# A third region of edges summed inside the scatter stage, and pairs that follow the tiles by six steps

## The reference

```python
edge_aggr = zeros.at[src].add(edge_attr).at[dst].add(edge_attr)   # layer 0
x += relu([relu(norm(x)), edge_aggr] @ W1 + b1) @ W2 + b2
agg = segment_sum(edge_attr, dst)                                  # layer 1
x += relu([relu(norm(x)), agg] @ W1 + b1) @ W2 + b2
x += gcn(relu(gcn(norm(x))))                                       # layer 2, degree-normalised
m = relu(concat(x[src], x[dst], edge_attr) @ msg_w1 + msg_b1) @ msg_w2 + msg_b2
x += relu([x, mean_by_dst(m)] @ upd_w1 + upd_b1) @ upd_w2 + upd_b2 # layer 3
```

## Time and profile before

| | before |
|---|---|
| time, median of 3 runs | 1234.61 us (1230.02 to 1240.17) |
| profiled execution, its own time | 1233.6 us |
| its span | 1231.7 us |
| PE, DVE, ACT, POOL busy | 1099.9, 894.7, 627.8, 703.4 us |
| granted clock of TensorE, mean | 0.949 |

### The profile page before, as it was taken

One profiled execution on the slowest core, in us unless ns is written; L12 is line 12 of the kernel. 1 busy time (PEld: TensorE's weight loads), 2 busy tenths in 40 slices (PEclk: granted clock), 3 DMA queues, 4 the chain that ended last, 5 costly groups with the idle time before them and its releaser, 6 DMA issues. The chain is left out here.

```text
span 1231.7 us, 31979 instructions
## 1 busy us (share of the span) xinstructions
PE 1099.9 (89%) x9535; PEld 934.9 (76%) x9536; DVE 894.7 (73%) x3140; ACT 627.8 (51%) x1794; POOL 703.4 (57%) x720
## 2 busy tenths in 40 slices
PE   6999896999998999926887999988799999999997
PEld 3666553888887888815854899973799999999985
DVE  7889775788877879876778754465577777777763
ACT  8666544889988788766632311043133333333322
POOL 4777777777777777781000000008577777777772
PEclk9999988999999999967988999988899999999997
DMA  7674334666555666445861000027878888788951
GB/s 237 191 224 134 106 106 129 159 162 157 154 157 158 186 184 197 146 129 164 242 8 48 2 1 2 2 73 213 224 215 220 230 227 236 216 239 230 232 132 49
DMA packets 177187, 188.62 MB, mean 153 GB/s; under 512 B 44320, under 2 KB 136845, under 8 KB 176877
## 3 DMA queue, kind: packets, MB, share of 16 engines
q1 hardware_dynamic: 142086, 136.92, 42.3%
q0 software_dynamic: 22656, 46.87, 12.5%
q10 hardware_dynamic: 12264, 2.70, 1.1%
HBM read 140.19 MB, written 44.28 MB: 150 GB/s over the span
## 5 line engine op out<-in xcount | busy, mean ns | idle before, releaser
L2605 POOL DMA_INDIRECT between<-p_table,src_g x292 | 285.4, 977 | 366.2 <-DMA p_table<-n_nm 269.4
L981 POOL DMA_INDIRECT rows_by_block<-h_t,mean_bc x312 | 312.3, 1001 | 105.3 <-issue 86.5
L471 PE MATMUL acc<-ones_b 128*128 128x128 bf16 (+1 forms) x941 | 162.0, 297 | 47.6 <-PEq L911 32.9
L1112 DVE TENSOR_TENSOR between<-between,acc 128x600 f32 x208 | 161.3, 776 | 50.2 <-PE acc L1266 38.6
L1255 PE MATMUL acc<-n_nm 128*128 128x384 bf16 (+1 forms) x832 | 143.0, 295 | 34.8 <-issue 21.9
L2744 ACT ACTIVATE between<-acc 128x128 f32<-128x128 f32 x138 | 38.2, 277 | 228.0 <-PE acc L2859 204.2
L1076 DVE TENSOR_SCALAR n_nm<-iota_w,agg_sum 128x600 bf16<-128x600 f16 x416 | 144.0, 387 | 0.0
L1000 ACT ACTIVATE away<-iota_b,agg_sum 128x128 bf16<-128x128 bf16 x416 | 140.8, 385 | 0.0
L1255 PEld LDWEIGHTS acc<-n_nm 128*128 128x128 bf16 x832 | 72.6, 98 | 82.6 <-issue 26.3
L471 PEld LDWEIGHTS acc<-ones_b 128*128 128x128 bf16 x941 | 73.8, 99 | 75.6 <-issue 58.3
L2842 PE MATMUL acc<-weights,between 128*128 128x128 f32 x584 | 128.4, 302 | 0.0
(11 more groups left out here) (296 smaller groups left out, 2553.9 us busy)
## 6 DMA issues: line engine op xcount, KB each, us to landing
h_t<-in_edge_rows SPq DMA_DIRECT2D x78, 260.0 KB
between<-in_edge_columns SPq DMA_DIRECT2D x36, 512.0 KB
between<-in_dst SPq DMA_DIRECT2D x36, 288.0 KB
n_nm<-rows_by_block SPq DMA_DIRECT2D x69, 130.0 KB
h_t<-rows_by_block SPq DMA_DIRECT2D x34, 260.0 KB, 3.8
by_dst<-q_whole_table SPq DMA_DIRECT2D x138, 64.0 KB
x_nm<-rows_by_block SPq DMA_DIRECT2D x30, 260.0 KB
agg_sum<-in_edge_rows SPq DMA_DIRECT2D x26, 260.0 KB
```

The costliest lines, as they stand in the source:

```text
L471: pe.matmul(acc[:, bank * BANK + skip:(bank + 1) * BANK].rearrange("p (a n) -> p a n", n=P), ones_b[:, :], ones_b[:, :].rearrange("p (a n) ...
L981: pool.indirect_dma_start(rows_by_block, bass.IndirectOffsetOnAxis(ap=place_in_table[:, t:t + 1], axis=0), row_group(g)[:, j, :], None).th ...
L1112: dve.tensor_tensor(between[:, :, bass.ds(first, W)], between[:, :, bass.ds(first, W)], acc[:, o:o + NB * WS].rearrange("p (b w) -> p b w" ...
L2605: pool.indirect_dma_start(got[:, q, j * D:(j + 1) * D], None, p_table, bass.IndirectOffsetOnAxis(ap=src_g[:, n * G + j:n * G + j + 1], axi ...
```

## The change

The table is cut into four regions: tiles to 124, 252, 356 and 416. The third one ("mid2", blocks of five or six tiles) is now read, summed and added to `held` inside the scatter stage too, by 25 more early reads at one per pair from pair 186 to 210; the loops of that stage run eight steps past the last pair for them. The earlier reads stand closer: the wide ones in 60 pairs instead of 68, the mid ones in 46 instead of 52. The last region has two to four tiles a block, so the source stage has 25 reads. x is also loaded once in the middle of the scatter stage, for its statistics, into the space that the early reads use afterwards (the load at the end stays). ACT checks nine blocks of counts at the end of the scatter stage and three in the source stage (five and 13 before), DVE combines 13 (seven before). `held` and `agg_dst` are added at the end of the scatter stage, some small works move there too (`oddities`), and the small works of the source stage stand earlier in it; the store of the keys stands behind SP's reads, with a wait for its landing. In the last stage the pairs follow the tiles by six steps (OFF) instead of ten, rows and keys of the first four batches are loaded ahead of the stores (their buffers are now in `held`), the late chunks stand in other steps, and two waits guard their buffers.

```diff
-TILES_MID = 256
+TILES_MID = 252
 GROUPS_MID = TILES_MID // KC
+TILES_MID2 = 356
+GROUPS_MID2 = TILES_MID2 // KC
...
+def cap_mid2(b):
+    return 6 if 15 <= b < 21 else 5 if b < NB - 1 else 3
...
-    return 7 if b < 15 else 8 if b < NB - 1 else 4
+    return 3 if b < 21 else 4 if b < NB - 1 else 2
...
-CHECKED_AT_END, CHECKED_BY_ACT = 5, 18
+CHECKED_AT_END, CHECKED_BY_ACT = 9, 12
...
+                reads.append((NSB + NB + b, base_mid2(b), cap_mid2(b), True, True))
...
-            TAILS = 7
+            TAILS = 11
             READS_AFTER = 4
+            AFTER_PAIRS = 8
+            X_LOAD_AT, X_ZERO_AT, X_STATS_AT = 30, 44, 58
...
-            read_pairs = {(78 + r * 68 // wide_reads if r < wide_reads else 148 + (r - wide_reads) * 52 // NB): r for r in range(len(early_reads))}
+            def pair_of_read(r):
+                if r < wide_reads:
+                    return 78 + r * 60 // wide_reads
+                if r < wide_reads + NB:
+                    return 140 + (r - wide_reads) * 46 // NB
+                return 186 + r - wide_reads - NB
...
+                            sp.wait_ge(x_stats.h, x_stats.at(2))
...
+                        if g == X_LOAD_AT:
+                            sp.wait_ge(vec.h, vec.at(1))
+                            sp.dma_start(x_nm[:, 0:NB - 1, :], x[0:(NB - 1) * P, :].rearrange("(b p) f -> p b f", p=P)).then_inc(x_in.h, 16)
+                            sp.dma_start(x_nm[0:NLAST, NB - 1, :], x[(NB - 1) * P:N, :]).then_inc(x_in.h, 16)
...
-                    for i in range((GROUPS - READS_AFTER) * PG, PAIRS):
+                    for i in range((GROUPS - READS_AFTER) * PG, PAIRS + AFTER_PAIRS):
...
-                    for i in range(PAIRS):
-                        lows(i)
+                    for i in range(PAIRS + AFTER_PAIRS):
+                        if i < PAIRS:
+                            lows(i)
...
+                        if X_STATS_AT <= i < X_STATS_AT + 13:
+                            for b in range(2 * (i - X_STATS_AT), min(2 * (i - X_STATS_AT) + 2, NB)):
+                                ins = dve.bn_stats(stats[:, b, :], x_nm[:, b, :])
...
+                        if i == PAIRS + 2:
+                            oddities()
...
-                    dve.wait_ge(loaded.h, loaded.at(16 * 23))
-                    for b in range(NB):
-                        dve.bn_stats(stats[:, b, :], x_nm[:, b, :])
+                    dve.wait_ge(agg_read.h, agg_read.at(NSB + 2 * NB))
+                    dve.tensor_tensor(held[:, :], held[:, :], agg_dst[:, 0:NSB * SBN], ALU.add)
...
-                        if r == 2 * LB_IN:
+                        if r == LB_IN + 1:
                             count_to_nodes(sp)
-                        if r == 4 * LB_IN:
+                        if r == LB_IN + 6:
                             nodes_in(sp)
-                        if r == 24:
-                            sp.wait_ge(keys_made.h, keys_made.at(4))
-                            sp.dma_start(keys_table[0:P, :, :], turned_keys[:, 0, :, :]).then_inc(keys_out.h, 16)
-                            sp.dma_start(keys_table[P:TILES_HERE, :, :], turned_keys[0:TILES_HERE - P, 1, :, :]).then_inc(keys_out.h, 16)
+                    sp.wait_ge(keys_made.h, keys_made.at(4))
+                    sp.dma_start(keys_table[0:P, :, :], turned_keys[:, 0, :, :]).then_inc(keys_out.h, 16)
+                    sp.dma_start(keys_table[P:TILES_HERE, :, :], turned_keys[0:TILES_HERE - P, 1, :, :]).then_inc(keys_out.h, 16)
+                    sp.wait_ge(keys_out.h, keys_out.at(32))
...
-                        c = u * P
-                        dve.wait_ge(agg_read.h, agg_read.at(2))
-                        dve.tensor_tensor(agg_sum[:, c:c + P], acc[:, o:o + P], agg_sum[:, c:c + P], ALU.add).then_inc(agg_read.h, 1)
+                        c, w = u * P, min(P, NSB * SBN - u * P)
+                        ins = dve.tensor_tensor(agg_sum[:, c:c + w], acc[:, o:o + w], held[:, c:c + w], ALU.add)
+                        if w < P:
+                            ins = dve.tensor_copy(agg_sum[:, c + w:c + P], acc[:, o + w:o + P])
+                        ins.then_inc(agg_read.h, 1)
...
-                    dve.tensor_tensor(agg_sum[:, 0:NSB * SBN], held[:, :], agg_dst[:, 0:NSB * SBN], ALU.add).then_inc(agg_read.h, 1)
-                    dve.tensor_copy(agg_sum[:, NSB * SBN:NP], agg_dst[:, NSB * SBN:NP]).then_inc(agg_read.h, 1)
...
-            OFF = 10
+            OFF = 6
...
-            p_win = table_space.take([P, PWINS, 2, D])
-            rows2 = table_space.take([P, BATCHES2 * 2, KW])
-            keys2 = table_space.take([P, BATCHES2, 2 * 2 * P], U8).rearrange("p r (j k e) -> p r j k e", j=2, k=2)
+            kept_space = Space(held[:, :], F32)
+            p_win = kept_space.take([P, PWINS, 2, D])
+            rows2 = kept_space.take([P, BATCHES2 * 2, KW])
+            keys2 = kept_space.take([P, BATCHES2, 2 * 2 * P], U8).rearrange("p r (j k e) -> p r j k e", j=2, k=2)
...
-            chunks = [(4, 42), (5, 58), (6, 74), (7, 90), (8, 106), (9, 122), (0, 133), (1, 135), (2, 137), (10, 139), (3, 141)]
+            chunks = [(4, 42), (5, 58), (6, 74), (7, 90), (8, 106), (9, 122), (0, 137), (1, 138), (10, 139), (2, 140), (3, 141)]
...
+                    def p_windows(b):
+                        u, r = 2 * b, b % BATCHES2
                         if starts(b):
...
+                    sp.wait_ge(keys_out.h, keys_out.at(32))
+                    for b in range(BATCHES2):
+                        tile_rows(b)
...
                     sp.wait_ge(p_stored.h, p_stored.at(TABLE_PARTS))
-                    sp.wait_ge(keys_out.h, keys_out.at(32))
-                    tile_rows(0)
-                    tile_rows(1)
+                    for b in range(BATCHES2):
+                        p_windows(b)
                     sp.wait_ge(q_stored.h, q_stored.at(2 * TABLE_PARTS))
-                    tile_windows(0)
-                    tile_windows(1)
-                    for b in range(2, BATCHES2):
-                        tile_rows(b)
+                    for b in range(BATCHES2):
                         tile_windows(b)
...
+                            if k >= 3:
+                                dve.wait_ge(hidden.h, hidden.at(k - 2))
...
+                            if k >= 3:
+                                act.wait_ge(made.h, made.at(second_of[k - 3] + 1))
```

More of the change, by code:

```diff
@@ L314, in build @@
         bases = sb("bases", [1, 2, NK])
-        over = Space(n_flat[:, 2944:NP], F32).take([1, 6, NB])
+        over = Space(n_flat[:, 2944:NP], F32).take([1, 8, NB])
         rel2 = sb("rel2", [P, TILES_HERE])
@@ L767, in build @@
         checked = signal("checked")
+        x_in, x_stats = tabs_in, idx_read
+        late = signal("late")
         early_away = of_block = signal("of_block")
@@ new lines, in oddities @@
+                    def oddities():
+                        lower1, upper1, lower_mid, upper_mid, lower_mid2, upper_mid2 = (bounds[:, k, :] for k in (0, 1, 4, 5, 6, 7))
+                        dve.scalar_tensor_tensor(pair_far[0:1, 0:PAIRS - RING].rearrange("p (a n) -> p a n", n=RING),
+                                                 iota[0:1, 0:PAIRS // RING - 1].rearrange("p (a n) -> p a n", n=1).broadcast_to([1, PAIRS // RING - 1, RING]), float(NODES_AT),
+                                                 win_f[:, RING:PAIRS].rearrange("p (a n) -> p a n", n=RING), ALU.mult, ALU.is_gt)
+                        dve.tensor_scalar(pair_far[0:1, PAIRS - RING:PAIRS - RING + PAIRS2], win_f[:, 0:PAIRS2], float(NODES2 - W), None, ALU.is_gt).then_inc(late.h, 1)
+                        dve.wait_ge(based.h, based.at(GROUPS))
+                        dve.tensor_tensor(over[:, 0, :], bases[:, GROUPS % 2, 0:NB], lower1, ALU.is_lt)
+                        dve.tensor_tensor(over[:, 1, :], bases[:, GROUPS % 2, 0:NB], upper1, ALU.is_gt)
+                        dve.tensor_tensor(over[:, 4, :], ends_mid[:, 0:NB], lower_mid, ALU.is_lt)
+                        dve.tensor_tensor(over[:, 5, :], ends_mid[:, 0:NB], upper_mid, ALU.is_gt)
+                        dve.tensor_tensor(over[:, 6, :], ends_mid2[:, 0:NB], lower_mid2, ALU.is_lt)
+                        dve.tensor_tensor(over[:, 7, :], ends_mid2[:, 0:NB], upper_mid2, ALU.is_gt).then_inc(late.h, 1)
+                        dve.wait_ge(late.h, late.at(1))
+                        dve.tensor_reduce(odd[0:1, 4:5], pair_far[0:1, 0:PAIRS - RING + PAIRS2], AX.X, ALU.add).then_inc(late.h, 1)
+                        dve.wait_ge(late.h, late.at(2))
+                        dve.tensor_reduce(odd[0:1, 3:4], over[:, :, :], AX.XY, ALU.add).then_inc(late.h, 1)
+                        dve.tensor_scalar(src_g[:, :], keys[:, 0, :], float(NP - 1), None, ALU.min)
+                        dve.wait_ge(late.h, late.at(4))
+                        dve.tensor_scalar(odd[0:1, 3:4], odd[0:1, 3:4], BIG, None, ALU.mult)
```

(12 more changed lines are left out.)

139 lines of the change are left out of this document (77 added, 62 removed).

## The result

The changed kernel takes 1255.85 us (median of 4, 1250.68 to 1261.03) against 1233.36 in the same comparison: 1.0187 times as long, 95% interval 1.0159 to 1.0215. I had said 1233, within 1214 to 1248. The profiled execution has a span of 1253.4 us against 1231.7, 21.7 more. Over the runs of this study the kernel before took 1226 to 1245 us, so single profiles of two kernels can differ by some 10 us for no reason of the code; I lean on medians, and on distances inside a stage.

What follows compares the result with a forecast made beforehand. The prediction took POOL to pace the scatter stage, row reads the source stage, and POOL to limit the last; +35 - 26 - 10 = -1 on the profiled 1233.6 gave 1232.6, stated as 1233 us, range 1214 to 1248.

Steps and rivals of the forecast that it cites:

- The list of what is last: Scatter stage's end: last sum at 571, then ACT done at 598, SP at 594, DVE at 590.
- ACT's share: Scatter stage's end: nine checks of 2.96 us, 28 us from ACT's last one-hots at 570 to 598.
- Pair 188 is collected at 489.1, two pairs more at most: Scatter stage: start of the added reads' delay, from which the last pair was put at 553 instead of 531.6.
- the slower rival: Closer reads eat PE's lead, scatter end +46, source stage gives 23, last stage 5: 1251 us, chance 0.18.
- On average 3.4: Scatter stage: us per pair with added reads; pairs 190 to 207 take 61 us.
- The ring: Scatter stage: buffers bind before the engines; 7.5 us from issue through ACT's one-hots and lows must fit into two pairs.
- The rival of the DMA queues: Scatter stage: POOL's long scatter comes from queue load, so the added x load costs up to 7 us; no chance given.
- The ring of six: Source stage: row reads turn in 5.5 us, 0.93 per read, 19.5 us for 21 reads; stage 32.5 us, -26.
- The term: Last stage: first add 12 us earlier, some given back, -10 us; at most -14, at least -4.
- the late chunks' waits: Last stage: the late node chunks' new waits are met in time; if not, 2 us.
- POOL's limit: Last stage: of POOL's 17.8 us of ring waits 8 can go; last add not before 1203 + 2, at most -14.
- +35: Scatter stage: the third region moves its end from 563.8 to 598.5 us; bounds +20 and +40.

Runs made afterwards that it cites:

- closer_reads_alone: The kernel before with the early reads as close as in the changed kernel, nothing else: 1233.52 us, ratio 0.9982 to the kernel before.
- four_row_buffers: The changed kernel with four row buffers instead of three and three one-hot buffers instead of two for the third region's reads: 1241.02 us, ratio 1.0076.
- lows_a_pair_ahead: The changed kernel with ACT making the next pair's lows ahead of the one-hots from pair 184 on: 1254.69 us, ratio 1.0203.
- three_hot_buffers: The changed kernel with three one-hot buffers instead of two for the third region's reads: 1257.23 us, ratio 1.0205.
- two_in_three_by_dve: The changed kernel with DVE making the one-hots of two third-region reads in three and ACT one: 1277.25 us, ratio 1.0337.

## Why the prediction was wrong

- **The scatter stage.** The list of what is last (sum, then ACT's nine checks, then SP, then DVE) was right, and so was ACT's share: 26 us from the last sum where I had 27.5. The last sum was 19.7 us late. Two steps failed, by 11 and 8 us in this profile.
- **"Pair 188 is collected at 489.1, two pairs more at most"** is the first: the forecast put the closer reads at nothing. Pair 189 was collected at 502.8, where the forecast's arithmetic has 492: 11 us. Some 3 of these are the profile that the forecast started from: in three others of the unchanged stage pair 189 stands at 494.5 to 495.3, where it has 491.4 (and at 499.2 to 502.8 in the six with the third region, three row buffers and ACT on two reads in three). I had the mechanism, as the slower rival: reads that come closer eat PE's lead over POOL, up to 10 us, and it decides if the lead at pair 186 is under 8 us. It was 4.2 (POOL ended pair 186 at 500.95). I gave it 0.18, on the thought that the middle reads would make part of it good. They made good 1.6 us of 13.3: from pair 138 to 186 PE is nearly at POOL's rate in both kernels. `closer_reads_alone` shows it with nothing else changed: the lead went and the time stayed, since POOL is last there. In the changed kernel the chain behind has no slack, so I count the lost lead in full; that it costs one for one there is my arithmetic, no run shows it alone.
- **"On average 3.4"** for a pair with a read is the second: 3.8 over the last 18 pairs, 8 us (6 to 9 in those six profiles). The ring does bind before the engines, as `four_row_buffers` shows, but I closed the loop through ACT alone. For one read in three it runs through DVE: landing, one-hots, a collect, the add, PE's next sum. 9.6 us from one sum to the next but one (552.5 to 562.1), where I had 7.5. The landing itself was well taken: 3.0 to 3.9 us from issue to the one-hots, in the four turns of the added reads in which they waited for their rows. A smaller slip: 1.42 us for a sum of six tiles, where the row shows 1.58, which is 0.14 us a pair on PE and changes no term. Nor do the added reads stand "where none were": before, six of the mid reads are issued at the pairs 187 to 197.
- **POOL.** Right on the scatter: none is long (1.67 at most), and the added load of x did nothing. In the five kernels in which DVE combines the counts while POOL still scatters there is one of 7.56 to 7.61 us, in the nine in which it starts later there is none; the two groups differ in more than that. The Trainium skill's rule that VectorE instructions with two SBUF inputs contend with GpSimd (GPSIMD Engine Reference, 1. Specifications) agrees with it. The rival of the DMA queues is out: in `closer_reads_alone` the long scatter lasts from 534.18 to 541.74, and the DMA engines move nothing in its second half (the last two columns):

```profile
538.00:541.70 3.70, 0.00 (x0) 0.00 (x0) 3.67 (x5) 3.67 (x3) 3.70 (x1) 0.50 0.00 0
```

- **The source stage.** -27.8 for -26. The ring of six is as worked out: SP waits 14.5 us for PE's sums, and 19 reads are issued from 622.4 to 638.5, 0.89 us each where I had 0.93.
- **The last stage.** The first add came 11.8 us sooner after the first window, as said. The term fell short by half, since 7 of these us were lost again by pair 110. I had listed the late chunks' waits and POOL's limit as what could come next, and edge loads only for the start. The instruction that I didn't follow is the load of the edges: SP issues it by the tile's step, and four steps less of lag take four pairs from its lead. POOL's limit was real too: it takes 375 us for its gathers where it took 382, so with the waits gone the last add could win some 11 us at most, not 14.
- **The sum and the chances.** -1 was a difference of two large terms of opposite sign, +35 and -26, of which the first hung on a lead that I had priced at nothing. The slower case had 0.18 and its 1251 was within 5 us, by half of its reasons and in part by luck: the lost lead was there, the landing of 4.2 us wasn't, and the turn through DVE took its place. The scatter stage lost 7 us more than its +46, and the source stage gave 5 more than its 23. The range ended below it.

## What to carry to other kernels

Work moved into the shadow of another engine is free only while the shadow lasts. Add up what each moved item costs per turn of its ring of buffers (here the 21 pairs took 74.9 us with reads and 37.8 without any, in `closer_reads_alone`, so 1.8 us for a read beside the pairs, and 2.7 for each of the seven sums behind them, against 1.2 that each read less gave back in the source stage), and take it from the slack at the place where it lands, with the lead that earlier items have already used.

When a wait for one buffer is relieved and the time stays, look at what the same instruction waits for now. Here the two buffers together gave 14 to 15 us, and the one-hots' buffer alone nothing that could be measured.

When a lag between two loops is shortened, every transfer of the later loop that is issued by the earlier loop's counter loses the same distance. List them before the sum is made.

## What was not expected of the hardware

A row read of five or six tiles that SP issues in the scatter stage took 3.6 us from issue to DVE's start in one turn (552.51 to 556.07) and 3.0 in another (575.23 to 578.21), hardly more than the 2.7 to 3.4 for the reads of up to four tiles in the next stage, though POOL scatters beside it.

TensorE lost its full clock twice inside the stretch that the ring paces. The same ten matmuls of a sum took 2.47 us right after PE had waited, at a granted clock of 0.50 (1.2 GHz), and 1.36 a few us later at 1.00 (2.4 GHz). Before the first fall, from 532.0 to 535.7, PE was busy for 2.3 of 3.7 us. The mean is 0.96 over the 76 us, where the kernel before has 1.00 from 485 to 532; by that mean some 6 us stood at the half clock, so PE's work took about 3 us longer, an estimate. Other versions of this stretch had less: 0.91 in `lows_a_pair_ahead`, 0.87 in `three_hot_buffers`, 0.82 in `two_in_three_by_dve`, where PE waited most. Waits in a loop can be paid a second time in this way.

```profile
535.73 2.47 PE L1319 MATMUL acc<-weights,x_nm 128*128 128x128 f32 x10 [0.89 <-DVE held L1176]
539.61 1.36 PE L1319 MATMUL acc<-weights,x_nm 128*128 128x128 f32 x10
```
```profile
535.73:538.20 2.47, 2.47 (x11) 2.35 (x12) 1.91 (x8) 0.00 (x0) 0.70 (x1) 0.50 0.06 22
539.61:541.00 1.39, 1.39 (x14) 1.27 (x14) 0.76 (x2) 1.36 (x5) 1.07 (x2) 1.00 0.67 248
```
